# Two layers of cross-attention and feed-forward on one core: three products moved to the end, an output chain five places later, nine norms' roots on GpSimd

## The reference

```python
x = x + L0_xattn(layernorm(x), ctx_4096, ...)   # 16 heads of 32, keys and values from a shared 32-wide latent
x = x + L0_ffn(layernorm(x), ...)               # x @ dequantised int4 weights + bias
x = x + L1_xattn(layernorm(x), ctx_4096, ...)   # 16 query heads, 4 key/value heads of 96, keys: ctx rows + own rows
x = x + L1_ffn(layernorm(x), ...)               # H + delta

# L1_ffn
H = x @ W.T + b
z = x @ A
H_scale = max(|H[:, 1::2, :8]|)                 # one maximum over ALL batches
d_scale = max(|z[:, 1::2] @ LiMEs.T|)           # the same
probs = softmax(0.5 * H_slice / H_scale + 0.5 * delta_slice / d_scale)
weights = probs * sigmoid((probs - second_largest) / 0.5), normalised, each used for two rows
delta = (z * (weights @ LiMEs)) @ Bmat * 0.5
```

## Time and profile before

| | us |
|---|---|
| median of 3 runs | 1970.17 (1968.33 to 1972.54) |
| the profiled execution | 1970.21 |
| its span (first to last recorded instruction) | 1968.4 |
| second block, 320 to 1010 | 690 |
| third block up to the last values' product, 1010 to 1909 | 899 |
| tail, 1909 to the end | 59 |

### The profile page before, as it was taken

One profiled execution on the slowest core, in us unless ns is written; L12 is line 12 of the kernel. 1 busy time (PEld: TensorE's weight loads), 2 busy tenths in 40 slices (PEclk: granted clock), 3 DMA queues, 4 the chain that ended last, 5 costly groups with the idle time before them and its releaser, 6 DMA issues. The chain is left out here.

```text
span 1968.4 us, 23187 instructions
## 1 busy us (share of the span) xinstructions
PE 1880.0 (96%) x8570; PEld 1334.5 (68%) x8570; DVE 1036.9 (53%) x1983; ACT 906.6 (46%) x1726; POOL 631.3 (32%) x504
## 2 busy tenths in 40 slices
PE   7999997999999999999899999999999999999997
PEld 6999894444466465555577777767776777767763
DVE  3564435667665665666525444564545455554414
ACT  2333331444344334434236666545655466645650
POOL 0000000000000000000027777757776577765760
PEclk9999995999999999999989999999999999999996
DMA  5978963000111020021177444435544145543101
GB/s 180 287 246 256 291 205 98 0 1 17 43 44 45 16 75 22 33 77 33 54 205 178 121 120 111 111 88 131 133 123 123 51 105 141 131 123 96 53 25 43
DMA packets 192950, 208.42 MB, mean 106 GB/s; under 512 B 87425, under 2 KB 157569, under 8 KB 192838
## 3 DMA queue, kind: packets, MB, share of 16 engines
q1 hardware_dynamic: 177124, 188.92, 33.7%
q10 hardware_dynamic: 15714, 18.03, 3.0%
HBM read 128.90 MB, written 77.94 MB: 105 GB/s over the span
## 5 line engine op out<-in xcount | busy, mean ns | idle before, releaser
L1417 POOL TENSOR_TENSOR pl<-pf,ph 128x512 fp32r<-128x512 f32 (+1 forms) x480 | 623.5, 1321 | 270.9 <-ACT pf L1607 270.3
L1604 ACT ACTIVATE ph<-ps 128x512 fp32r<-128x512 f32 (+1 forms) x480 | 288.1, 600 | 369.8 <-PE ps L1504 309.7
L1690 DVE TENSOR_REDUCE pm<-ps 128x1 f32<-128x464 f32 x480 | 299.8, 636 | 203.0 <-PE ps L1435 199.6
L1140 DVE TENSOR_REDUCE pm<-ps 128x1 f32<-128x400 f32 (+3 forms) x544 | 285.3, 572 | 90.8 <-PE ps L987 86.8
L1047 ACT ACTIVATE pr<-ps 128x512 f32<-128x512 f32 (+1 forms) x416 | 219.6, 600 | 196.0 <-PE ps L919 195.2
L1607 ACT ACTIVATE pf<-ps 128x512 f32<-128x512 f32 (+1 forms) x480 | 289.1, 602 | 3.3 <-POOL pl L1417 2.5
L1406 POOL MEMSET vh<- 128x30 f32 x1 | 0.2, 154 | 700.3 <-POOLq L684 700.3
L932 PE MATMUL ps<-pr,cv 128*64 128x512 f32 (+1 forms) x832 | 210.6, 622 | 0.0
L1522 PE MATMUL ps<-ph,vh 128*97 128x512 f32 (+1 forms) x480 | 191.4, 399 | 0.0
L1525 PE MATMUL ps<-pl,vh 128*97 128x512 f32 (+1 forms) x480 | 190.1, 396 | 1.1 <-POOL pl L1417 0.8
L1523 PE MATMUL ps<-ph,vl 128*97 128x512 f32 (+1 forms) x480 | 189.2, 394 | 0.0
(11 more groups left out here) (264 smaller groups left out, 3104.0 us busy)
## 6 DMA issues: line engine op xcount, KB each, us to landing
woT<-wo_turned SPq DMA_DIRECT2D x30, 768.0 KB, 6.0
v_scr<-vst SPq DMA_DIRECT2D x16, 1152.0 KB
cnat<-in_ctx_dram SPq DMA_DIRECT2D x16, 768.0 KB
q_scr<-qst SPq DMA_DIRECT2D x48, 256.0 KB, 2.5
vh<-v_scr SPq DMA_DIRECT2D x15, 672.0 KB
vl<-v_scr SPq DMA_DIRECT2D x15, 672.0 KB
home<-k_scr SPq DMA_DIRECT2D x14, 696.4 KB, 8.4
k_scr<-home SPq DMA_DIRECT2D x24, 384.0 KB, 7.8
```

The lines of the kernel that those rows point to most:

```text
L1140: dve.reduce_max(pm[:, j, ch:ch + 1], src[:, 0:(cuts if s < S else next_cuts)[ch][1]], AX)\
L1417: pool.tensor_tensor(pl[0:m, n % 2, cols], pf[0:m, half, :], ph[0:m, n % 2, cols].bitcast(F32), ALU.subtract).then_inc(plo, 1)
L1604: act.activation(ph[0:keys[kt], n % 2, cols], src, ACT.Exp, scale=S1).then_inc(phi, 1)
L1690: ins = dve.reduce_max(pm[:, j, ch:ch + 1], at[:, 0:cuts[ch][1]], AX)
```

## The change

Five edits.

1. Of the six `h` products of batches 0 to 2, three leave the groups: (2, 0), (2, 1) and (1, 1). The first stands in the tail ahead of `sum`, the other two behind the `out` items, ahead of batch 3's `turn`. To keep their input, the turned rows have two buffers (`xT_of`), and those of batch 3 lie in `orec`, which is made wider.
2. In `beside(s)` the step `invert` goes from place 6 to 11, `normal` from 17 to 23, `low` from 39 to 42, and the `stacked` items from 41 and 45 to 43 and 46. ScalarE's five steps go from behind the tiles 2, 3, 6, 7, 9 to 4, 5, 7, 8, 10.
3. The norm is cut into `norm_stats`, `norm_root` and `norm_apply`. The root's guess takes one instruction on the pair where three led to it, and the two additions of EPS are one, behind both aggregations: 11 small instructions in place of 13.
4. For nine norms of the second block (batches 0 to 2, and the three `xa`) the root runs on GpSimd as 14 instructions (`pool_root`). VectorE signals the statistics, reads four more ring items, waits for the root, and applies it.
5. W's product for batch 3 is split: 4 products where 8 stood, 2 behind the turn of the weights, and 2 behind the mixture's product. `ol` is computed ahead of the ring items of the tail.

```diff
+def pool_root(pool, chain, mv, v, t, y):
+    chain.link(pool.tensor_scalar(v[:, :], mv[:, :, 1], EPS, None, ALU.add))
+    chain.link(pool.tensor_scalar(y[:, :].bitcast(I32), v[:, :].bitcast(I32), -0.5, RSQRT_GUESS, ALU.mult, ALU.add))
+    for i in range(3):
+        chain.link(pool.tensor_tensor(t[:, :], y[:, :], y[:, :], ALU.mult))
+        chain.link(pool.tensor_tensor(t[:, :], t[:, :], v[:, :], ALU.mult))
+        chain.link(pool.tensor_scalar(t[:, :], t[:, :], -0.5, 1.5, ALU.mult, ALU.add))
+        last = pool.tensor_tensor(y[:, :], y[:, :], t[:, :], ALU.mult)
...
+            roots = Chain(pool, step_r, 0)
+            for n in range(3 * (B - 1)):
+                pool.wait_ge(stats_done, n + 1)
+                pool_root(pool, roots, ln["mv"], ln["v"], ln["t"], ln["y"]).then_inc(root_done, 1)
...
+            def begin_norm(x_rows, out, chain_of, ready):
+                norms[0] += 1
+                norm_stats(dve, chain_of, x_rows, ln["st"], ln["mv"], pause).then_inc(stats_done, 1)
+                waiting.append([4, norms[0], x_rows, out, chain_of, ready])
+            def end_norm():
+                _, n, x_rows, out, chain_of, ready = waiting.pop()
+                dve.wait_ge(root_done, n)
+                norm_apply(dve, chain_of, out, x_rows, ln["mv"], ln["y"], pause).then_inc(ready, 1)
...
+    LATE = [(B - 2, 0), (B - 2, 1), (1, 1)]
...
-                return [("sum", s - 1, 0)] + [("out", s - 1, i) for i in range(TT * G)]
+                return [("h", *LATE[0]), ("sum", s - 1, 0)] + [("out", s - 1, i) for i in range(TT * G)]
...
+            later = [None if item and item[0] == "h" and item[1:] in LATE else item for item in later]
...
-            order = most[:6] + own[:1] + most[6:14] + later[:2] + own[1:2] + most[14:19] + later[2:3] + most[19:23] + later[3:4] + most[23:26] + later[4:6] + \
-                most[26:28] + later[6:] + [None, None] + own[2:] + [None]
+            order = most[:11] + own[:1] + most[11:13] + later[:2] + most[13:17] + [None] + most[17:19] + own[1:2] + [None] + \
+                later[2:3] + most[19:22] + [None] + most[22:24] + later[3:4] + most[24:26] + later[4:6] + most[26:28] + \
+                later[6:] + [None, None] + own[2:]
             for i in range(NO):
-                order += [("stacked", s - 1, i), most[28 + 2 * i], None, most[29 + 2 * i]]
+                order += [("stacked", s - 1, i)] + most[28 + 2 * i:30 + 2 * i]
...
-            for t in range(TT):
-                for c in range(DC):
-                    pe.matmul(bank(t), xT[:, c, t * P:(t + 1) * P], w1T[:, c, :], start=(c == 0), stop=False)
+            own(0, 0, DC)
             pe.wait_ge(to_pe, 3)
...
+            own(1, 0, DC // 2)
             pe.wait_ge(to_pe, 4)
...
+            own(1, DC // 2, DC)
...
-                        step = {2: send_parts, 3: spread_parts, 6: send_o, 7: stack_o, 9: stacked_hi}.get(kt)
+                        step = {4: send_parts, 5: spread_parts, 7: send_o, 8: stack_o, 10: stacked_hi}.get(kt)
```

More of the change, by code:

```diff
@@ L60, in link, with norm_stats @@
         self.engine.wait_ge(self.sem, self.base + self.n)
-def layernorm(dve, chain, out, x, st, mv, v, t, u, y, pause=lambda: None, between=lambda: None):
+def norm_stats(dve, chain, x, st, mv, between=lambda: None):
     between()
@@ L71, in layernorm, with norm_root, norm_apply @@
     chain.link(dve.bn_aggr(mv[:, 0, :], st[:, 0, :]))
-    chain.mark(dve.tensor_scalar(v[:, 0:1], mv[:, 0, 1:2], EPS, None, ALU.add))
-    chain.link(dve.bn_aggr(mv[:, 1, :], st[:, 1, :]))
-    chain.link(dve.tensor_scalar(v[:, 1:2], mv[:, 1, 1:2], EPS, None, ALU.add))
-    chain.link(dve.tensor_scalar(t[:, :].bitcast(I32), v[:, :].bitcast(I32), 1, None, ALU.logical_shift_right))
-    chain.link(dve.tensor_scalar(y[:, :].bitcast(I32), t[:, :].bitcast(I32), -1.0, RSQRT_GUESS, ALU.mult, ALU.add))
-    for _ in range(3):
-        pause()
-        chain.link(dve.tensor_tensor(t[:, :], y[:, :], y[:, :], ALU.mult))
-        chain.link(dve.scalar_tensor_tensor(u[:, :], t[:, :], -0.5, v[:, :], ALU.mult, ALU.mult))
-        chain.link(dve.scalar_tensor_tensor(y[:, :], u[:, :], 1.5, y[:, :], ALU.add, ALU.mult))
+    return dve.bn_aggr(mv[:, 1, :], st[:, 1, :])
+def norm_root(engine, chain, mv, v, t, u, y, pause=lambda: None):
+    chain.link(engine.tensor_scalar(v[:, :], mv[:, :, 1], EPS, None, ALU.add))
+    chain.link(engine.tensor_scalar(y[:, :].bitcast(I32), v[:, :].bitcast(I32), -0.5, RSQRT_GUESS, ALU.mult, ALU.add))
+    for i in range(3):
+        pause()
+        chain.link(engine.tensor_tensor(t[:, :], y[:, :], y[:, :], ALU.mult))
+        chain.link(engine.scalar_tensor_tensor(u[:, :], t[:, :], -0.5, v[:, :], ALU.mult, ALU.mult))
+        last = engine.scalar_tensor_tensor(y[:, :], u[:, :], 1.5, y[:, :], ALU.add, ALU.mult)
+        if i < 2:
+            chain.link(last)
+    return last
+def pool_root(pool, chain, mv, v, t, y):
+    chain.link(pool.tensor_scalar(v[:, :], mv[:, :, 1], EPS, None, ALU.add))
+    chain.link(pool.tensor_scalar(y[:, :].bitcast(I32), v[:, :].bitcast(I32), -0.5, RSQRT_GUESS, ALU.mult, ALU.add))
+    for i in range(3):
+        chain.link(pool.tensor_tensor(t[:, :], y[:, :], y[:, :], ALU.mult))
+        chain.link(pool.tensor_tensor(t[:, :], t[:, :], v[:, :], ALU.mult))
+        chain.link(pool.tensor_scalar(t[:, :], t[:, :], -0.5, 1.5, ALU.mult, ALU.add))
+        last = pool.tensor_tensor(y[:, :], y[:, :], t[:, :], ALU.mult)
+        if i < 2:
+            chain.link(last)
+    return last
+def norm_apply(dve, chain, out, x, mv, y, between=lambda: None):
     last = None
@@ L88, in layernorm @@
     return last
-LN_STEPS = 6 + 2 + 9 + TT - 1
+def layernorm(dve, chain, out, x, st, mv, v, t, u, y, pause=lambda: None, between=lambda: None):
+    chain.link(norm_stats(dve, chain, x, st, mv, between))
+    chain.link(norm_root(dve, chain, mv, v, t, u, y, pause))
+    return norm_apply(dve, chain, out, x, mv, y, between)
+LN_STEPS = 4 + 2 + 9 + TT - 1
 def shift_rows(dve, rows, turned, negid):
@@ L1233, in grouped_attention @@
         pf = sb("pf", [P, 2, BANK])
-        xT = sb("xT1", [P, DC, T])
+        xTs = sb("xT1", [P, 2, DC, T])
         x = sb("x1", [P, B, TT, D])
@@ L1311, in last_batch @@
             e = B - 1
-            return [("turn", e, 0), ("turn", e, 1), ("z", e, 0), ("h8", e, 0), ("dl", e, 0)]
+            return [("h", *late) for late in LATE[1:]] + [("turn", e, 0), ("turn", e, 1), ("z", e, 0), ("h8", e, 0), ("dl", e, 0)]
         def delta_bank(n):
@@ L1564, in _, with own @@
             pe.matmul(bank(3)[:, 0:2], ones2[:, :], dg[:, :], start=True, stop=True).then_inc(from_pe, 1)
-            for t in range(TT):
-                for c in range(DC):
-                    pe.matmul(bank(t), xT[:, c, t * P:(t + 1) * P], w1T[:, c, :], start=(c == 0), stop=False)
+            def own(t, c0, c1):
+                for c in range(c0, c1):
+                    pe.matmul(bank(t), xT_of(B - 1)[:, c, t * P:(t + 1) * P], w1T[:, c, :], start=(c == 0), stop=False)
+            own(0, 0, DC)
             pe.wait_ge(to_pe, 3)
```

39 lines of the change are left out of this document (24 added, 15 removed).

## The result

| us | before | after |
|---|---|---|
| median (range, runs) | 1971.28 (1968.33 to 1972.54, 4) | 1948.83 (1945.41 to 1952.13, 4) |
| ratio | | 0.9887, 95% interval 0.9866 to 0.9909 |
| profiled execution / its span | 1970.21 / 1968.4 | 1948.22 / 1946.4 |

The change makes the kernel about 22 us faster; 38 were forecast. The two profiled executions can be cut at the same instructions. The second block runs here from its first score product to that of its last group, the third from the first values' product of group 0 to that of group 15.

The account below looks back on a forecast made before the run. TensorE, busy 96% of the span, was taken as the bound, with time won from its work, waits and clock. From 1970.2 us, 10.3 + 6 + 3.5 + 11 + 7 = 37.8 came off: forecast 1932 us, range 1915 to 1950.

Parts of the forecast that it names:

- Three `h` products, 10.3 us: Third block: three items of 3.44 us each leave the groups, where TensorE is the bound, saving 10.3 us.
- The output chain, 6: Third block outside the norms: five places later, the chain's waits go, saving 6 us, range 0 to 12.
- Rival C: Third block: the `stacked` item comes too early for `low`, its wait returns at place 43; 1952 us, chance 0.07.
- The norms of groups 5, 9 and 13, 3.5: Third block: 1.2 us saved a norm, 3.5 in all, bounds -3 and 9.3.
- Nine roots on GpSimd, 11: Second block: 9 us for waits and 2 for the clock, 11 saved, range 2 to 22, cost taken as 0.
- rival A: Second block gives nothing, since VectorE keeps statistics, applications and additions and waits for the roots; 1943 us, chance 0.12.
- The first call on GpSimd: First of the nine roots: freshly loaded code costs about 6 us once, stalling VectorE some 2 to 4 us.
- The tail, 7: From the last values' product on: four terms sum to 7.2 us, taken as 7, range 0 to 10.
- (a): Tail: an `h` item in the wait for the sums keeps TensorE's clock up through the `out` products, saving 3.0 us.
- (b): Tail: two other `h` products, 6.9 us, run while TensorE waits for the norm; 0 net.
- (c): Tail: TensorE comes warm into `z` and the products behind it, saving 1.8 and an estimated 0.9 us.
- (d): Tail: with W's product split, mixture weights to first last product takes 5.4 us instead of 6.95, saving 1.5.

Follow-up runs that it names:

- e4: Changed kernel with the three `h` products back in groups 9 and 13 and none in the tail: 1964.98 us, ratio 0.9968.
- e3: Changed kernel with the output chain at its old places and ScalarE's steps behind their old tiles: 1955.07 us, ratio 0.9908.
- e5: Changed kernel with one empty place put back at place 6 of groups 5, 9 and 13, where `invert` had stood: 1945.66 us, ratio 0.9874.
- e7: Changed kernel with VectorE's root written column by column in one-element forms, 22 small instructions instead of 11: 1949.9 us, ratio 0.9882.
- e1: Changed kernel, but VectorE counts eight ring items instead of four before it waits for GpSimd's root: 1943.15 us, ratio 0.9856.
- e10: Changed kernel with six ring items instead of four before the root's wait, and an empty place at place 6 of groups 5, 9, 13: 1936.43 us, ratio 0.9824.
- e12: Changed kernel with the second half of W's product in one piece again, ahead of the mixture's product: 1949.27 us, ratio 0.9892.
- e11: Changed kernel with eight ring items, an empty place 6 and a one-element-form root in groups 5, 9, 13 only: 1939.92 us, ratio 0.9855.
- e8: Changed kernel with eight ring items, four empty places moved into the norms of groups 5, 9, 13, and VectorE's root in one-element forms: 1945.83 us, ratio 0.9877.
- e2: Changed kernel with the nine roots back on VectorE: 1949.3 us, ratio 0.9887.

## Why the prediction was right, and where it was not

The sign, and a time inside the range, came out (1948.8 in 1915 to 1950). The time is 1.2 us from the range's slow end, and single executions went up to 1952.13, so that it lies inside is in part luck. The likeliest case, 1932, was two terms too good: they were forecast as 14.5 us together and gave -1.3. Of the signs named, GpSimd's pace, the `stacked` item, ScalarE's wait and the clock up to 1918 came as forecast; VectorE's wait for the root (2.5 us, not under 2) did not, nor did TensorE's own waits in the third block (8.2 us for VectorE's reads, where 11.2 stood).

- **Three `h` products, 10.3 us: right.** e4 has 11.75 us more in groups 9 and 13. In group 13 it is 7.15 for two items, 6.9 by the forecast; in group 9 4.60 for one, with the clock at half for 6.8 us instead of 3.4.
- **The output chain, 6: right.** The eleven groups without a norm lost 5.0 us, and 6.5 come with e3. ScalarE's wait is gone, and at `stacked` no wait came. Rival C did not happen.
- **The norms of groups 5, 9 and 13, 3.5: wrong sign.** Without the items that left, they got 7.50 - 10.32 = 2.8 us longer. The failed step is "I take 1.2 us a norm": it counts waits and instructions, with "`invert` is no longer among the seven items" as a relief of VectorE, and has no term for the clock. The relief was real but small. TensorE's third wait (1.16 us in group 5) is gone and its second is longer, 1.52 for 0.83, since the place of `invert` was empty for TensorE, a breath in which VectorE caught up, and a maximum stands there now. In the three groups it stands 1.5 us less. What turned the sign is the clock: at half for 13.6 us in the three groups, where before it never fell. Its price can be read in group 5, which has the same waits in five profiles: 68.23 us with no half clock (e4; 68.60 before), 69.2 and 69.3 with 3.4 us of it, 70.1 and 70.2 with 6.8. That is about 0.95 us for each 3.4, so by an estimate from these rows 3.8 us for 13.6, and without it the norms would have given some 1.0 us. e5 gives back 2.6 of the 2.8 (70.09 + 66.20 + 62.42 less 68.72 + 65.59 + 61.84), with more waiting and no half clock; 1.2 of it, in groups 9 and 13, is nearly the same in every profile with the same items, and 1.4 lies in group 5, where the clock makes it vary. The Trainium skill's rule on the shared port (SBUF — State Buffer, "Who interferes with whom"), used in the prediction, held (L76 1.21 and L80 1.20 us here). In e7 the instructions of one element, with or without a scalar from memory, run through at 0.14 to 0.27 us.
- **Nine roots on GpSimd, 11: failed, 1.5.** The duration was well estimated (3.4 us for 3.8). What failed is "four ring items stand between ... and the ring of four banks hides that". Three stand between: the item at which the norm begins is counted as the first, and the fourth in the order comes behind the wait. They take 0.5 us each, so VectorE stood for 2.5 us, not 1.5, and TensorE felt it. And at two of the nine norms there was little to gain, since VectorE waits for ScalarE there. That a read at 1.07 us paces the items was true only while VectorE had a root to do between them. e1 and e10 (6.3 and 8.4 us from a number) show that the gain of 11 was there to be had: 9.9 against before in e10. It is rival A's outcome. A had named the wait for the roots, but for the reason that TensorE's wait lies ahead of them, which e1 and e10 exclude. Whether six items beat eight is less sure: 0.5 to 2.3 us, from one profile with six.
- **The first call on GpSimd.** By the Trainium skill (GPSIMD Engine Reference, "2.1 Instruction dispatch") the first call of freshly loaded code would cost about 6 us once. In this case's trace the first root begins at 412.12, 0.36 us behind the start of the last aggregation (411.76), and VectorE's wait there is 2.59 us, 0.1 more than at the others. It takes 3.80 us, like the others. So no such cost shows at the first arithmetic instruction here.
- **The tail, 7: right in sum (7.9), by its terms only in part.** (a) From group 15's first values' product to the last `out` read it went from 59.0 (1923.15 - 1864.14) to 56.2 us (1906.16 - 1849.97): 2.8 for 3.0. (b) The turn waited for the `h` items until 1912.01, 0.8 us behind the norm's end, as foreseen. (c) `z` is 1.89 for 3.59, 1.7. From the last `out` read to L1620 it is 12.4 us for 15.3, so (b) and (c) gave 2.9 for 2.7. (d) 6.4 us from the weights (1925.8) to the first last product, where 5.4 were expected and 6.95 stood before: 0.5 for 1.5, and e12 measures 0.5 as well. The clock fell at 1918.3, in the waits ahead of the mixture's weights. W's first product took 5.91 us at half clock and still held TensorE when the weights were ready, so L1630 began 0.65 us behind them. The two pieces ran at full clock but took 1.9 us each, not 1.7. The clock was up from 1925.1 to 1935.4, which made the stretch from the first last product to the end 1.6 us shorter (14.15 for 15.77). The prediction had no term for that; that the sum is right is luck by this much.

What stays open: why the clock falls behind the same two waits in one execution and not in another; how GpSimd's subtractions could be kept off VectorE's applications (e11); and why the queries come late to the first group in e8.

## What to carry to other kernels

When work is handed to a second engine to be fetched a few steps later, count the steps that truly stand between hand-over and wait, at the first engine's *relieved* pace, and put more there than the second engine's time needs, but not so many that the next consumer waits for the result: four gave nothing, eight 6 to 8 us, six 8. In a list that paces two engines, a step that is empty for the faster one is slack that something may live on; moving it away is an edit of its own. Less waiting in sum is no gain by itself: here two waits, one of them longer, in place of three cost more, by the clock behind them, than the waiting that was saved. Work that fills a real idle stretch in a tail pays twice, since the clock then stays up for what follows.

## What the runs showed of the hardware

- GpSimd executes a dependent chain of [128, 2] instructions at 0.19 us each, 0.27 from start to start; the very first took 0.22.
- The same two waits of TensorE, 1.09 and 1.52 us with products between them, are followed by half clock for 6.8 us (changed kernel, e2), for 3.4 (e1, e12) or not at all (e4). Group 5 took 70.1 and 70.2, 69.3 and 69.2, and 68.2 us: the clock alone makes 2 us in one place, and so a part of the spread between executions.
- In groups 5, 9 and 13 of the profiles, no half clock came in the 15 groups where TensorE's longest wait was 1.27 us or less (before, e3, e5, e7, e10), though it stood up to 3.5 us in all. It came in 22 of the 24 where one wait was 1.46 us or more, with 2.0 to 3.4 us in all. The two that stayed at full clock are group 5 of e4 (1.52) and group 9 of e8 (2.01). The orders of the items differ too, so this is no proof that the longest wait is the cause.
- VectorE's small instructions with two elements a row take up to 1.22 us beside GpSimd's subtractions and 0.16 without; those of one element take 0.14 to 0.27 in both cases (e7).
